# Table stage of a graph-attention kernel: Wq loaded and turned first, loads reordered, some subtractions on GpSimd

## The reference

```python
vcq = jnp.concatenate([exp_v, q_exp], axis=-1)
self_feat = vcq @ W_self.T + b_self
kv = self_feat[:, :ng]
qh = (self_feat @ Wq.T + bq).reshape(B, N, H, dh)
kh = (kv @ Wk.T + bk).reshape(B, ng, H, dh)
aff = jnp.einsum('bnhd,bmhd->bnhm', qh, kh) * (1.0 / np.sqrt(dh))
...
mod = jax.nn.silu(c) @ W_mod + b_mod
```

## Time and profile before

| what | before |
| --- | --- |
| median of 3 runs | 2940.2 us (2939.44 to 2941.28) |
| profiled execution, its own time | 2935.65 us |
| profiled execution, span | 2933.8 us |
| granted TensorE clock, mean | 0.992 of full |
| TensorE busy | 98% |
| VectorE, ScalarE, GpSimd busy | 76%, 55%, 35% |

### The profile page before, as it was taken

One profiled execution on the slowest core, in us unless ns is written; L12 is line 12 of the kernel. 1 busy time (PEld: TensorE's weight loads), 2 busy tenths in 40 slices (PEclk: granted clock), 3 DMA queues, 4 the chain that ended last, 5 costly groups with the idle time before them and its releaser, 6 DMA issues.

```text
span 2933.8 us, 68348 instructions
## 1 busy us (share of the span) xinstructions
PE 2866.5 (98%) x27842; PEld 2453.5 (84%) x27842; DVE 2216.9 (76%) x2956; ACT 1609.6 (55%) x3284; POOL 1040.8 (35%) x675
## 2 busy tenths in 40 slices
PE   8999999999999999999999999999999999979998
PEld 6888889999887777777777777777788999979998
DVE  4789886555546888888888888888577777567876
ACT  2666653332214777777777777777233656544442
POOL 1112110000002444444444444447566555563332
PEclk9999999999999999999999999999999999989999
DMA  7222236553695433333333333332664555577775
GB/s 238 89 88 74 87 135 226 203 216 104 226 312 143 117 88 88 92 91 88 92 92 88 95 88 88 100 94 70 213 227 162 198 205 201 217 241 236 243 242 173
DMA packets 273905, 445.07 MB, mean 152 GB/s; under 512 B 34569, under 2 KB 149417, under 8 KB 270025
## 3 DMA queue, kind: packets, MB, share of 16 engines
q1 hardware_dynamic: 264740, 434.48, 45.8%
q0 software_dynamic: 576, 6.29, 0.5%
q10 hardware_dynamic: 8292, 0.05, 0.2%
HBM read 266.99 MB, written 173.74 MB: 150 GB/s over the span
## 4 chain that ended last, share of the span: by engine, by line
PE 61%; DMA 2%; POOL 2%; DVE 2%; ACT 1%; issue 1%; SPq 1%; POOLq 0%; ACTq 0%; DVEq 0%
PE b_po L1850 16%; PE b_ps L1821 13%; PE b_tp_act L1833 8%; PE d_pm L2515 8%; PE d_pm L2527 4%; PE c_po L2102 4%; PE d_spare L2527 3%; PE d_pt L2527 3%; PE b_tp_dve L1833 2%; PE d_spare L2515 1%; DMA c_ot<-o_t 1%; POOL d_blocks L2374 1%; POOL w_raw L113 1%; DMA hidden_blocks<-d_blocks 0%; DMA d_x_second_raw<-hidden_blocks 0%
## 5 line engine op out<-in xcount | busy, mean ns | idle before, releaser
L1878 DVE TENSOR_REDUCE head_nm<-b_ps 128x1 f32<-128x1024 f32 x510 | 599.5, 1217 | 16.5 <-PE b_ps L1821 3.3
L1789 ACT ACTIVATE b_p<-b_ps,head_nm 128x1024 f32<-128x1024 f32 x510 | 562.7, 1113 | 0.0
L1850 PE MATMUL b_po<-b_pt,b_v 128*64 128x256 f32 x4096 | 498.4, 385 | 0.8 <-DVE b_pt L1898 0.8
L1794 ACT ACTIVATE b_pt<-b_tp_act 128x512 f32<-128x512 f32 x512 | 308.3, 602 | 306.9 <-PE b_tp_dve L1833 306.9
L1898 DVE COPY b_pt<-b_tp_dve 128x512 f32<-128x512 f32 x512 | 351.6, 687 | 116.7 <-PE b_tp_dve L1833 116.6
L1833 PEld LDWEIGHTS b_tp_act<-ident,b_p 64*128 64x128 f32 x4096 | 311.2, 138 | 120.0 <-issue 100.4
L1850 PEld LDWEIGHTS b_po<-b_pt,b_v 128*64 128x64 f32 x4096 | 272.0, 136 | 128.5 <-ACT b_pt L1794 0.9
L1833 PE MATMUL b_tp_act<-ident,b_p 64*128 64x64 f32 x4096 | 347.4, 225 | 2.4 <-issue 2.4
L1833 PE MATMUL b_tp_dve<-ident,b_p 64*128 64x64 f32 x4096 | 347.9, 225 | 0.0
L1833 PEld LDWEIGHTS b_tp_dve<-ident,b_p 64*128 64x128 f32 x4096 | 311.6, 138 | 13.0
L2374 POOL TENSOR_TENSOR d_blocks<-d_blocks 128x512 f32<-128x512 f32 x128 | 189.7, 1482 | 114.5 <-ACT d_blocks L2426 107.6
(11 more groups left out here) (443 smaller groups left out, 7643.1 us busy)
## 6 DMA issues: line engine op xcount, KB each, us to landing
b_raw_q<-q_t SPq DMA_DIRECT2D x124, 256.0 KB, 4.2
x_mlp_raw<-hidden_blocks SPq DMA_DIRECT2D x112, 256.0 KB, 3.7
d_x_second_raw<-hidden_blocks SPq DMA_DIRECT2D x112, 256.0 KB, 3.3
hidden_blocks<-d_blocks SPq DMA_DIRECT2D x32, 768.0 KB, 3.3
k_t<-p_out SPq DMA_DIRECT2D x64, 256.0 KB, 2.2
q_t<-p_out SPq DMA_DIRECT2D x64, 256.0 KB, 2.3
v_n<-p_out SPq DMA_DIRECT2D x64, 256.0 KB, 4.1
b_v<-v_n SPq DMA_DIRECT2D x32, 512.0 KB, 3.9
```

What stands on the lines that cost most here:

```text
L1789: act.activation(pr[k % 4][:], ps[k % 2][:], ACT.Exp, bias=nm[:, k % 4:k % 4 + 1], accum_out=rs[:, n:n + 1]).then_inc(exp_done, 1)
L1794: act.activation(dst, src, ACT.Copy).then_inc(t_out[0], 1)
L1850: mm = pe.matmul(po[rows, (blk % 2) * 2 * P:(blk % 2 + 1) * 2 * P], vt[u][:, kc, rows], pt[blk % 2][h][:, kc, :], start=(kc == 0), stop=(k ...
L1878: dve.tensor_reduce(nm[:, k % 4:k % 4 + 1], ps[k % 2][:], axis=AX.X, op=ALU.max, negate=True).then_inc(max_done, 1)
```

## The change

It has these parts. `wq` is loaded first, in two halves with a semaphore each, and TensorE turns it first; half of `ws_t` comes after `x` and `cond`. Its transposes rotate over four PSUM banks. The load of `b_mod` counts on `s_in`, with the other small vectors, and both waits on `s_in` ask for all six. The load of `w_mod` waits for `ws_n` instead of `wk`. The turning of `css` comes after `sf_t`. Tile 0's transposes, copy and subtraction sit in the large product, at `j == 4`. GpSimd makes three of the four `gl` and also `cgl`; ScalarE makes `cgh`, after slot 3.

```diff
-        WQT_BANK = (2, 3, 4, 6, 5, 0, 1, 2)
+        WQT_BANK = (2, 3, 4, 6, 2, 3, 4, 6)
         SF_BANK = (3, 4, 6, 5)
...
             ws_parts = t["ws_t"].rearrange("(k p) n -> p k n", p=P)
-            sp.dma_start(ws_t[:, KC:, :], ws_parts[:, KC:, :]).then_inc(ws_in, 16)
+            for d in range(2):
+                sp.dma_start(wq[:, d], t["wq"][d].rearrange("(k p) n -> p k n", p=P)).then_inc(wq_in[d], 16)
             for b in range(B):
...
                 sp.dma_start(xkv[rows, F:2 * F], t["cond"][b:b + 1, :].to_broadcast([M0, F])).then_inc(x_in, 16)
-            sp.dma_start(wq[:], t["wq"].rearrange("d (k p) n -> p d k n", p=P)).then_inc(wq_in, 16)
+            sp.dma_start(ws_t[:, KC:, :], ws_parts[:, KC:, :]).then_inc(ws_in, 16)
             sp.dma_start(ws_t[:, 0:KC, :], ws_parts[:, 0:KC, :]).then_inc(ws_x_in, 16)
...
             act.dma_start(rowb[B:B + 1, 1:3, :], t["bout"].rearrange("(a d) n -> a d n", a=1)).then_inc(s_in, 16)
-            act.dma_start(b_mod[:], t["b_mod"].rearrange("(k p) -> p k", p=P), allow_slow_non_contiguous=True).then_inc(b_mod_in, 16)
-            act.wait_ge(ct_in, 16)
-            act.activation(silu_t[:, :, 0:B], c_t[:], ACT.Silu).then_inc(silu_done, 1)
+            act.dma_start(b_mod[:], t["b_mod"].rearrange("(k p) -> p k", p=P), allow_slow_non_contiguous=True).then_inc(s_in, 16)
             for j in range(2 * KC):
...
                 act.copy(wqt_h[:, j, :], ps[WQT_BANK[j]]).then_inc(wqt_high, 1)
-            act.wait_ge(s_in, 16 * 5)
+            act.wait_ge(ct_in, 16)
+            act.activation(silu_t[:, :, 0:B], c_t[:], ACT.Silu).then_inc(silu_done, 1)
+            act.wait_ge(s_in, 16 * 6)
             for n in range(KC):
...
                                        ).then_inc(first.sum_done, 1)
+                if j == 4:
+                    act.wait_ge(first.xt_done, 1)
+                    act.copy(first.xh[:, 0:F], ps[2])
+                    act.copy(first.xh[:, F:], ps[3][:, 0:P]).then_inc(first.xh_copied, 1)
                 if j == 3:
...
                     act.copy(first.gh[:, ic, :], raw[:, slot_of(0), ic * A0:(ic + 1) * A0]).then_inc(gh_done, 1)
-            act.wait_ge(first.xt_done, 1)
-            act.copy(first.xh[:, 0:F], ps[4])
-            act.copy(first.xh[:, F:], ps[5][:, 0:P]).then_inc(first.xh_copied, 1)
+                if s == 3:
+                    act.wait_ge(cg_written, 2)
+                    act.copy(cgh[:], cgs[:]).then_inc(cg_written, 1)
 
...
             pool.memset(y5[:], 0.0).then_inc(pool_done, 1)
-            pool.wait_ge(wk_in, 16)
+            pool.wait_ge(ws_n_in, 16)
             for k in range(KC):
...
                 pool.memset(first.x5[k][:, F + 1:F + 4:2], 1.0).then_inc(first.zeros, 1)
+            for ic in range(KC - 1):
+                pool.wait_ge(gh_done, ic + 1)
+                pool.tensor_tensor(first.gl[:, ic, :], raw[:, slot_of(0), ic * A0:(ic + 1) * A0], first.gh[:, ic, :],
+                                   ALU.subtract).then_inc(gl_done, 1)
+                if ic == 1:
+                    pool.wait_ge(cg_written, 3)
+                    pool.tensor_tensor(cgl[:], cgs[:], cgh[:], ALU.subtract).then_inc(cg_written, 1)
 
...
 
+            pe.wait_ge(id_ready, 2)
+            for j in range(2 * KC):
+                if j % KC == 0:
+                    pe.wait_ge(wq_in[j // KC], 16)
+                if j >= 4:
+                    pe.wait_ge(wqt_rest, j - 3)
+                for c in range(KC):
+                    mm = pe.transpose(ps[WQT_BANK[j]][:, c * P:(c + 1) * P], wq[:, j // KC, j % KC, c * P:(c + 1) * P], ident[:])
+                mm.then_inc(wqt_done, 1)
             pe.wait_ge(ws_in, 16)
...
             mm.then_inc(q_done, 1)
-            pe.wait_ge(id_ready, 2)
             pe.wait_ge(dve_step, 4)
...
             mm.then_inc(xt_done, 1)
-            pe.wait_ge(wq_in, 16)
-            for j in range(2 * KC):
-                if WQT_BANK[j] == 5:
-                    pe.wait_ge(css_done, 3)
-                if WQT_BANK[j] < 2:
-                    pe.wait_ge(xt_copied, WQT_BANK[j] + 1)
-                if j == 7:
-                    pe.wait_ge(wqt_rest, 1)
-                for c in range(KC):
-                    mm = pe.transpose(ps[WQT_BANK[j]][:, c * P:(c + 1) * P], wq[:, j // KC, j % KC, c * P:(c + 1) * P], ident[:])
-                mm.then_inc(wqt_done, 1)
-            for n in range(KC):
-                mm = pe.transpose(ps[7][:, n * TW:n * TW + B], css[0:B, n * P:(n + 1) * P], ident[0:B, 0:B])
-            mm.then_inc(q_done, 1)
             pe.wait_ge(ws_x_in, 16)
             pe.wait_ge(xt_copied, 2)
+            pe.wait_ge(wqt_rest, 2 * KC)
             for n in range(KC):
-                pe.wait_ge(wqt_rest, n + 2)
+                if n == KC - 1:
+                    pe.wait_ge(css_done, 3)
                 for k in range(2 * KC):
...
                 mm.then_inc(sf_done, 1)
+            for n in range(KC):
+                mm = pe.transpose(ps[7][:, n * TW:n * TW + B], css[0:B, n * P:(n + 1) * P], ident[0:B, 0:B])
+            mm.then_inc(q_done, 1)
             pe.wait_ge(wk_in, 16)
             pe.wait_ge(sf_copied, KC)
-            pe.wait_ge(wqt_rest, 2 * KC)
             for dc in range(2 * KC):
...
                     modulation(MOD_AT[j])
+                if j == 4:
+                    pe.wait_ge(first.rs_done, 1)
+                    pe.wait_ge(kb_written, 8 * KC)
+                    for c in range(KC):
+                        pe.transpose(ps[2][:, c * P:(c + 1) * P], first.x5[0][:, c * P:(c + 1) * P], ident[:])
+                    pe.transpose(ps[3][:, 0:P], first.x5[0][:, F:], ident[:]).then_inc(first.xt_done, 1)
                 if j == 6:
+                    pe.wait_ge(first.xl_done, 1)
                     pe.wait_ge(mod_rows_done, 2)
...
             slot_free(6)
-            pe.wait_ge(first.rs_done, 1)
-            for c in range(KC):
-                pe.transpose(ps[4][:, c * P:(c + 1) * P], first.x5[0][:, c * P:(c + 1) * P], ident[:])
-            pe.transpose(ps[5][:, 0:P], first.x5[0][:, F:], ident[:]).then_inc(first.xt_done, 1)
             for m, part in enumerate((2, 5)):
...
         def _(dve):
+            for j in range(2 * KC):
+                dve.wait_ge(wqt_high, j + 1)
+                dve.tensor_tensor(wqt_l[:, j, :], ps[WQT_BANK[j]], wqt_h[:, j, :], ALU.subtract).then_inc(wqt_rest, 1)
             dve.wait_ge(x_in, 16 * 2 * B)
...
                                 ps[hf].rearrange("p (k r) -> p k r", r=P)[:, :, 0:R0]).then_inc(xt_copied, 1)
-            dve.wait_ge(s_in, 16 * 5)
+            dve.wait_ge(s_in, 16 * 6)
             dve.wait_ge(q_done, 1)
...
             dve.tensor_copy(css[0:B, :], ps[5][0:B, :]).then_inc(css_done, 1)
-            for j in range(2 * KC):
-                dve.wait_ge(wqt_high, j + 1)
-                dve.tensor_tensor(wqt_l[:, j, :], ps[WQT_BANK[j]], wqt_h[:, j, :], ALU.subtract).then_inc(wqt_rest, 1)
             dve.wait_ge(css_done, 3)
...
             dve.sem_inc(first.adj_used, 1)
-            dve.wait_ge(b_mod_in, 16)
+            dve.wait_ge(first.xh_copied, 1)
+            dve.tensor_tensor(first.xl[:], ps[2], first.xh[:, 0:F], ALU.subtract).then_inc(first.xl_done, 1)
             for part in (1, 4):
...
                         dve.tensor_copy(dst[:, :, e], ps[e][:, 0:GC].rearrange("r (h b m) -> r h b m", h=H0 // NT, b=B)).then_inc(cg_written, 1)
-                    dve.wait_ge(cg_written, 2)
-                    dve.tensor_copy(cgh[:], cgs[:]).then_inc(cg_written, 1)
-                    dve.wait_ge(cg_written, 3)
-                    dve.tensor_tensor(cgl[:], cgs[:], cgh[:], ALU.subtract).then_inc(cg_written, 1)
-                if d:
+                if s == SLOTS - 1:
                     dve.wait_ge(gh_done, ic + 1)
...
                                       ALU.subtract).then_inc(gl_done, 1)
-            dve.wait_ge(first.xh_copied, 1)
-            dve.tensor_tensor(first.xl[:], ps[4], first.xh[:, 0:F], ALU.subtract).then_inc(first.xl_done, 1)
             for m in range(2):
```

More of the change, by code:

```diff
@@ L266, in graph_tables @@
             "act_out dve_out gh_done gl_done")
-        (id_ready, b_mod_in, silu_done, mod_done, mod_t_done, mod_rows_done, mod_rows_t, gates_done, gates_copied) = sems(
-            chain, nc, "tables", "id_ready b_mod_in silu_done mod_done mod_t_done mod_rows_done mod_rows_t gates_done gates_copied")
-        ws_in, ws_x_in, ws_n_in, wk_in, wq_in, wo_in, css_out, out_done, gates_out = sems(
-            chain, nc, "tables", "ws_in ws_x_in ws_n_in wk_in wq_in wo_in css_out out_done gates_out")
+        (id_ready, silu_done, mod_done, mod_t_done, mod_rows_done, mod_rows_t, gates_done, gates_copied) = sems(
+            chain, nc, "tables", "id_ready silu_done mod_done mod_t_done mod_rows_done mod_rows_t gates_done gates_copied")
+        ws_in, ws_x_in, ws_n_in, wk_in, wo_in, css_out, out_done, gates_out = sems(
```

(2 more changed lines are left out.)

## The result

The changed kernel took 2958.7 us in the median of 4 runs (2956.6 to 2960.6), the kernel before 2939.8 (4 runs, its profiled one among them): ratio 1.0071, 95% interval 1.0060 to 1.0083. The profiled execution took 2956.6, 21.0 more than that of before. The forecast was 2958.0, in a range from 2946 to 2965. The sum came out, but three of its four terms did not.

A forecast was written before the change was run, and what follows sets the result against it. TensorE, busy 98% of the span, was taken as the bound, so delays move all that follows. Head 10.4, transposes 0.6, table chain 5.1 and clock 1.7 sum to 17.8 us; from the median of 2940.2: 2958.0, range 2946 to 2965.

The forecast's parts named there:

- The landing of `b_mod`: In the head: queues alternate packets one for one, so `b_mod` lands at 32.3 us and starts the head's path.
- I expect no hole: In the head's loads: with `wq` ahead of `x` and `cond`, SyncE's queue stays loaded, without its earlier gap at 6 to 8 us.
- Rival 1: In the head: `b_mod` isn't late, as 4-byte packets go more than one to a turn; +4.5 to +6.2 us; chance 0.10.
- From that landing to the large product: In the head: 23.6 us, 1.7 of it for the lower clock, starting the large product at 55.9, 10.4 us later.
- Tile 0's transposes: In the large product: five transposes put between products that TensorE does without a pause, +0.6 us.
- The table chain: Before the first logits: `cgl` on GpSimd ends 5.1 us later, and 12.3 us of writing and fetching follow unchanged.
- The slots' evacuation: In the slots: with VectorE relieved, it ends about 3.5 us sooner but gains nothing, as TensorE waits ahead of `logits(0)`.
- The clock at the logits: At the first tile's logits: TensorE's clock falls in a wait of some 9 us, +1.7 us, between 0 and 3.
- Rival 2: Before the logits: fetches shrink in a quieter stage, so `logits(0)` comes with the evacuation; +7.5 us, 2947.7; chance 0.05.
- Rival 3: In the stages after the logits: later TensorE waits take up all 17.8 us, so 2940, no change; chance 0.04.
- Rival 4: In the head's loads: `b_mod` meets `w_mod`'s longer rows and lands 10 us later, 2968; chance 0.05.
- Rival 5: In head and table chain: neither delay is real and the faster evacuation remains; -4.1 us, or 2936; chance 0.03.

The follow-up runs named there:

- e4: Changed kernel with 48 transposes of Wq, which nobody reads, on TensorE ahead of its wait for `css_done`: 2949.5 us, ratio 1.0042.
- e2: Changed kernel with `b_mod` counted on another semaphore, so nothing ahead of `sf_t` waits for it: 2945.9 us, ratio 1.0030.
- e1: Kernel before with only the load of `b_mod` counted on `s_in` and both waits asking for all six: 2965.2 us, ratio 1.0096.
- e3: Changed kernel with `cgh` and `cgl` on VectorE again, as in the kernel before: 2953.9 us, ratio 1.0053.
- e6: Kernel before with only tile 0's transposes in the large product and GpSimd's three `gl`: 2939.0 us, ratio 1.0001.
- e7: Changed kernel with 72 filler transposes of the identity in the wait before the logits: 2956.2 us, ratio 1.0058.
- e10: Changed kernel with 36 filler transposes of the identity in the wait before the logits: 2955.7 us, ratio 1.0062.

## Why the prediction was right, step by step

**The landing of `b_mod`** was forecast at 32.3 and came at 33.2. The reasoning by alternating packets held: 342 to 343 packets from 6 to 8 us, 357 to 355 from 28 to 30. Only "I expect no hole" did not: one came from 8 to 12 us. The equal counts alone would fit turns of ten and ten as well as of one and one; the packets' start times in the trace of the kernel before tell them apart. Of the 368 small packets of 14 to 16 us, 298 are followed exactly 6 ns later by the start of one of SyncE's packets, and 29 by that of another small one. The rule of the Trainium skill (DMA: Bandwidth & Descriptors, "Queues, rings and completion order"), by which an engine drains typically 9 to 17 descriptors of a queue at a turn, is not what these times show, where each packet is one row or one element. Rival 1 fell.

**From that landing to the large product** the sum had 23.6 us; it took 29.7. This is the term that was mis-sized, the 1.7 for the clock: "if it lasts to 5, that is 2.5" allowed a short fall of the clock, and it lasted past 55. At the lower level `kh` took 13.91 us, more than VectorE's 10.50 for `kb`, so TensorE set the pace of a stage that VectorE had set. e4 shows this: the clock kept up, the same wait left in place, the product starts at 55.2. The wait is not the only way to the fall (in e2's profile the clock fell without it), nor does a fall in the wait always last to `kh` (in e1's it did not). What decides how long it lasts stays open. The head came to 17.5 us instead of 10.4.

**Tile 0's transposes** were forecast at 0.6: the large product to the slots takes 29.32 us instead of 28.74.

**The table chain** was forecast at 5.1 and was worth 2.6. `cgl` came 4.9 us later after the slots' start, as forecast, with GpSimd's 1.54 and 1.55 as in the earlier trace rows. The step that failed was "the 12.3 us of writing and fetching follow unchanged": they took 10.0. Of the 2.3 us less, 0.8 are in the writing: from `cgl`'s end to the first fetch it took 4.1 instead of 4.9. Another 1.3 are in the fetching: by the landings in the two traces the last one came 5.84 us after the first fetch was issued (106.80 to 112.64), before 7.10 (84.60 to 91.70). And some 0.2 were not the chain's at all: in the kernel before, the product at 92.00 had stood behind `xl`, which ended at 91.85. Why the same fourteen fetches land sooner is not shown; in e3 and e6, where the slots run beside them as before, they took 6.65 and 7.25.

**The slots' evacuation** was read as VectorE's. A row of the kernel before that I had not drawn on shows more: behind one wait for VectorE the clock fell, and four of the eight products ran at the lower level, TensorE busy throughout.

```profile
81.34 7.29 PE L424 MATMUL g_ps<-g_kb,g_m 32*128 32x80 f32 x128 [1.66 <-DVE g_raw L621]
...
81.40:88.60 7.20, 7.20 (x129) 7.01 (x129) 4.73 (x10) 3.72 (x8) 0.00 (x0) 0.50 0.09 20
```

In the changed kernel's profile all eight ran at the upper level (2.03 us for each pair), and the last `gh` starts 11.7 us after the slots' start instead of 15.5. The forecast had 3.5 sooner, but not for this reason: TensorE's last four products took 4.1 us there instead of 7.3. It takes the splits' move away from VectorE: in e3 and e6, which leave them there, TensorE waits 2.04 and 2.05 us for VectorE and four of the eight run at the lower level again (7.13). Nor is it sure: in the profiles of e7 and e10, whose slots are the changed kernel's, the last two products took 3.71 and 3.72.

**The clock at the logits** was forecast at 1.7: the first tile's group took 2.1 us longer than before, and e10 gets it back. It leaves no trace in the end: from the logits to the span's end it is 2842.1 us against 2841.8, and further on the clock falls again for short stretches that differ between the two (from 2600 to 2650 us it is 0.83 in the mean before and 0.90 after). So 0.3 is left of this term's 1.7.

**Nothing is taken up later.** The logits start 20.7 us late, the first projection 20.8 (439.7 against 418.9), the span ends 21.0 late. Rivals 2, 3, 4 and 5 fell. Hidden, as forecast, were the turning of Wq, ScalarE's hold, and the load of the modulation weights.

The errors were +7.1 (head), -2.5 (table chain) and -1.4 (clock at the logits): they sum to 3.2, which is 21.0 less 17.8. That they have opposite signs is luck; the mechanism of the largest term, the wait for `b_mod` and its landing, was right, and what the clock makes of that wait was mis-sized. The median hit closer than the profiled run, since its distance to the profiled run was 2.1 us after and 4.5 before. The forecast of 2958.0 owes some 2 us to this, which is luck too: the median of 2940.2 that it started from is of three runs, and the 76 runs beside the experiments have 2937.8.

## What to carry to other kernels

A semaphore that counts several transfers waits for the slowest. Before a transfer joins such a count, look up when it lands, and what kind of packets it has beside those it shares the engines with. And price an idle TensorE by the work that follows it: here the wait stood ahead of 20 us of work that then ran at the lower clock, and of the 17.5 us that the head lost, some 7 were the clock's (e4: the large product 7.7 us sooner, 0.45 of it by the landing). A cheap filler shows in one run how much of a loss is wait and how much is clock.
